# Moving evictions and two K jobs inside the attention pair loop of a fused two-layer kernel

## The reference

```python
x = x + tanh(g_xattn[0]) * L0_xattn(layernorm(x), ctx, ctx, mask, Wq, bq, Wk, bk, Wv, bv)
x = x + tanh(g_ffn[0])   * L0_ffn(layernorm(x), w1, w2, h1, h2, w3)          # ternary weights
x = x + tanh(g_xattn[1]) * L1_xattn(layernorm(x), ctx, ctx, Wq, bq, Wk, bk, Wv, bv, Wo, bo)
x = x + tanh(g_ffn[1])   * L1_ffn(layernorm(x), w_gate, w_up, w_down)        # rounded activations
# attention: scores = q @ k.T / sqrt(32); p = softmax(scores); out = p @ v, per batch and head
```

## Time and profile before

| what | value |
| --- | --- |
| median of three runs | 1588.3 us |
| the profiled execution | 1586.92 us |
| its span in the profile | 1584.5 us |
| PE busy | 1565.0 us, 99% |
| DVE, ACT, POOL busy | 1026.0, 971.0, 423.9 us |
| DMA, mean | 165 GB/s |

### The profile page before, as it was taken

One profiled execution on the slowest core, in us unless ns is written; L12 is line 12 of the kernel. 1 busy time (PEld: TensorE's weight loads), 2 busy tenths in 40 slices (PEclk: granted clock), 3 DMA queues, 4 the chain that ended last, 5 costly groups with the idle time before them and its releaser, 6 DMA issues.

```text
span 1584.5 us, 25762 instructions
## 1 busy us (share of the span) xinstructions
PE 1565.0 (99%) x9322; PEld 1427.5 (90%) x9322; DVE 1026.0 (65%) x1815; ACT 971.0 (61%) x2014; POOL 423.9 (27%) x569
## 2 busy tenths in 40 slices
PE   9999999999999999999999999999999999999999
PEld 7899899889888999999999998889999989988765
DVE  6577887787785563223544325647777777778987
ACT  5576777677665455444544435446677767666676
POOL 4121221222134222222222222311211121123751
PEclk9999999999999999999999999999999999999999
DMA  7766767677582325554365652576676677667500
GB/s 244 189 169 168 196 176 195 162 203 182 137 218 83 99 89 188 176 195 161 99 228 195 222 162 90 176 187 172 161 195 174 167 189 179 172 147 209 197 13 30
DMA packets 149974, 261.28 MB, mean 165 GB/s; under 512 B 41137, under 2 KB 94001, under 8 KB 149710
## 3 DMA queue, kind: packets, MB, share of 16 engines
q1 hardware_dynamic: 149505, 259.24, 58.3%
q10 hardware_dynamic: 332, 0.23, 0.0%
HBM read 191.01 MB, written 58.57 MB: 158 GB/s over the span
## 4 chain that ended last, share of the span: by engine, by line
PE 87%; DVE 6%; ACT 3%; DMA 2%; issue 1%; POOL 1%; SPq 0%; DVEq 0%; ACTq 0%
PE ps L1218 33%; PE ps L852 14%; PE ps L856 13%; PE ps L952 7%; PE ps L930 6%; PE ps L1152 2%; PE ps L1018 2%; PE ps L914 2%; PE ps L919 1%; DVE nmax L1367 1%; PE ps L1169 1%; PE ps L872 1%; ACT P L1909 1%; DVE PT L1373 1%; DMA kd<-ksl 1%
## 5 line engine op out<-in xcount | busy, mean ns | idle before, releaser
L1218 PE MATMUL ps<-ah_f,wh_f 128*128 128x400 f32 (+1 forms) x1296 | 442.9, 343 | 0.0
L1218 PE MATMUL ps<-al_f,wh_f 128*128 128x400 f32 (+1 forms) x1296 | 442.2, 342 | 0.0
L2272 POOL TENSOR_TENSOR cxl<-raw,cxh 128x384 fp32r<-128x384 f32 (+1 forms) x112 | 105.7, 965 | 562.7 <-ACT cxh L1851 562.7
L1773 DVE TENSOR_TENSOR wl_f<-raw_f,wh_f 128x1024 fp32r<-128x1024 f32 x85 | 103.7, 1223 | 231.9 <-POOL wh_f L2262 231.8
L1218 PEld LDWEIGHTS ps<-al_f,wh_f 128*128 128x128 f32 x1296 | 243.8, 188 | 0.0
L1218 PEld LDWEIGHTS ps<-ah_f,wh_f 128*128 128x128 f32 x1296 | 243.5, 188 | 0.1
L1367 DVE TENSOR_REDUCE nmax<-ps 100x1 f32<-100x722 f32 x256 | 220.6, 902 | 35.0 <-PE ps L918 31.4
L1909 ACT ACTIVATE P<-ps,nmax 100x722 f32<-100x722 f32 x256 | 219.9, 862 | 30.1 <-DVE nmax L1367 30.1
L1921 ACT ACTIVATE PT<-ps 128x400 fp32r<-128x400 f32 x384 | 165.9, 505 | 70.4 <-PE ps L930 69.2
L2190 ACT ACTIVATE raw_f<-wl_f 128x1024 f32<-128x1024 f32 x88 | 93.4, 1061 | 173.6 <-DVE wl_f L1773 173.0
L1373 DVE TENSOR_TENSOR PT<-ps,PT 128x400 fp32r<-128x400 f32 x384 | 196.3, 566 | 4.3 <-ACT PT L1921 1.1
(11 more groups left out here) (226 smaller groups left out, 2665.2 us busy)
## 6 DMA issues: line engine op xcount, KB each, us to landing
KS<-kd SPq DMA_DIRECT2D x192, 361.0 KB
raw_f<-in_h SPq DMA_DIRECT2D x64, 512.0 KB, 3.9
raw_f<-in_gud SPq DMA_DIRECT2D x48, 512.0 KB, 4.3
raw<-in_ctx SPq DMA_DIRECT2D x64, 192.0 KB, 3.6
raw_f<-in_w SPq DMA_DIRECT2D x24, 512.0 KB, 3.9
kd<-ksh SPq DMA_DIRECT2D x60, 192.0 KB, 2.2
kd<-ksl SPq DMA_DIRECT2D x60, 192.0 KB, 2.5
raw<-in_ctx SPq DMA_DIRECT2D x64, 169.0 KB, 4.5
```

Of the source, the lines that this page charges most:

```text
L1218: return e.matmul(o, p, q, start=start, stop=stop)
L1773: e.tensor_tensor(wl[:, z, :], raw[:, r, :], raw32(wh[:, z, :]), ALU.subtract).then_inc(v_ul, 1)
L2272: e.tensor_tensor(m.cx[1][:, k, off:off + n], m.raw[:, k, off:off + n], raw32(m.cx[0][:, k, off:off + n]), ALU.subtract).then_inc(g_cx, 1)
```

## The change

It has five parts.

1. `BESIDE[4]`: in pairs with `p == 4` K(2,0) comes first and K(0,1) second, before it was the other way. This holds for batches 1 to 7, so for seven pairs (4, 12, ... 52) in each layer, on every engine and in SyncE's stores.
2. The tail of batch 0 (and 1) is made in pair 0, behind K(3,1), in place of pair 1 ahead of its V job.
3. ScalarE evicts the tails of the other pairs (9, 17, 33, 41, 49 in both layers) between the two exponentials, not behind both.
4. The normalized rows of batch 5 are turned in pair 58, not 57; `normal_out` for them is in pair 57, not 56, and `keep_normal` in pair 58, behind both exponentials.
5. In pair 57 of the first layer VectorE does `low_weighed(55)` ahead of both maxima, not between them.

```diff
-          (("k", 1, 0, 1), ("k", 1, 2, 0)),
+          (("k", 1, 2, 0), ("k", 1, 0, 1)),
...
 def tail_at(i):
-    return i // 8 if i < NP and i % 8 == 1 and i // 8 % 4 < 3 else None
+    return i // 8 if i < NP and (i == 0 or i > 8 and i % 8 == 1) and i // 8 % 4 < 3 else None
...
     if i == NP - 1:
         return KEPT
-    return i // 8 - 2 if i % 8 == 1 and 16 < i < NP else None
+    if i == NP - 6:
+        return KEPT - 1
+    return i // 8 - 2 if i % 8 == 1 and 16 < i < NP - 8 else None
...
 # TensorE (JOBS, RINGS, VectorE and ScalarE: low_tail(0), high_tail(0) stand behind the jobs in the same way)
-                    if tail_at(i) is not None:
+                    if i and tail_at(i) is not None:
                         tail_job(tail_at(i))
                     for j in beside(i):
                         job(j)
+                    if i == 0:
+                        tail_job(0)
...
 # VectorE
-                    early = scaled_at(i) is not None or L == 0 and i < NP - 7 and (
-                        out_at(i) is not None or turned_at(i) is not None)
-                    between = L == 0 and i == NP - 7
+                    early = scaled_at(i) is not None or L == 0 and (i == NP - 7 or i < NP - 7 and (
+                        out_at(i) is not None or turned_at(i) is not None))
...
-                    if L == 0 and i == NP - 8:
+                    if L == 0 and i == NP - 7:
                         normal_out(i // 8 - 2)
...
 # ScalarE
                     if i + 1 < NP:
                         weights(2 * i + 2)
+                    if i and tail_at(i) is not None:
+                        high_tail(tail_at(i))
                     if len(beside(i)) < 2 and i + 1 < NP:
                         weights(2 * i + 3)
-                    if L == 0 and i == NP - 7:
+                    if L == 0 and i == NP - 6:
                         keep_normal(turned_at(i))
                     if L == 0 and i == NP - 1:
                         high_normal(KEPT)
-                    if tail_at(i) is not None:
-                        high_tail(tail_at(i))
...
                     for j in beside(i)[1:]:
                         high_job(j)
+                    if i == 0:
+                        high_tail(0)
```

More of the change, by code:

```diff
@@ L160 @@
     for _l in range(2):
-        if tail_at(_i) is not None:
+        if _i and tail_at(_i) is not None:
             JOBS[_l].append(("v", tail_at(_i), KT - 1))
         JOBS[_l] += beside(_i)
+        if _i == 0:
+            JOBS[_l].append(("v", 0, KT - 1))
         if scaled_at(_i) is not None:
@@ L169 @@
             RINGS[_l].append(("xn", turned_at(_i)))
-        if tail_at(_i) is not None:
+        if _i and tail_at(_i) is not None:
             RINGS[_l].append(("v", tail_at(_i), KT - 1))
         RINGS[_l] += beside(_i)
+        if _i == 0:
+            RINGS[_l].append(("v", 0, KT - 1))
         if _l and _i in OUT_AT:
@@ L1625, in attention @@
                         peak(2 * i + 2)
-                        if between:
-                            low_weighed(i - 2)
                         peak(2 * i + 3)
-                    if i >= 2 and not early and not between and (L == 0 or i < NP):
+                    if i >= 2 and not early and (L == 0 or i < NP):
                         low_weighed(i - 2)
@@ L1651, in attention @@
                         low_job(j)
+                    if i == 0:
+                        low_tail(0)
                     if L == 0 and out_at(i) is not None:
```

## The result

The kernel after takes 1592.41 us (median of 9 runs, 1590.87 to 1595.94), the kernel before 1587.81 (9 runs, 1585.70 to 1588.71): ratio 1.0033, 95% interval 1.0024 to 1.0043. It is slower by 4.6 us; forecast were 4.1 us more and 1592.4. The profiled execution took 1592.31 us with a span of 1589.9, before 1586.92 and 1584.5.

A forecast was written before the change was run, and what follows sets the result against it. TensorE is busy 99% of the span, so only edits moving a matmul's start count. Terms +9.3 - 1.7 - 1.4 - 1.2 - 0.9 = +4.1 us gave 1592.4 us, range 1586.5 to 1596.5.

The forecast's parts named there:

- Part 1, added: Pairs p = 4: K(2,0), now first, waits for K(1,0)'s store, issued behind spread_q, and delays the V product; +9.3 us.
- the nine named: Pairs forecast to stall: 4, 28, 36, 44 of the first layer; 4, 12, 28, 36, 44 of the second; 9.3 us.
- D - (end of job B) + 1.63: Stall cost in a pair p = 4, not under 0; D is when K(1,0)'s second transfer lands, job B the second K job.
- the six pauses: Pauses of about 1 us within SyncE's issues in six of nine stalling pairs, expected again; 6.0 us of the cost.
- The slow landings: Late-landing K(1,0) stores behind the other three stalls in pairs p = 4; 3.4 us, which may fall elsewhere.
- Rival (b): No change: pauses in SyncE's issues stay, slow landings do not; 6.0 - 5.2 = +0.8 us, 1589.1; chance 0.30.
- Part 1, removed: Stalls in pair 21 of the first layer and 53 of the second vanish as K(2,0)'s store leaves earlier; -1.7 us.
- Rival (c): Much slower: K(0,.) loads from p = 4 also miss pair 7, and pair 0's tail gains nothing; +10.5 us, 1598.8; chance 0.07.
- Part 2: Tail in pair 0: pair 2's transposes start at 72.0 instead of 72.69; 0.7 us in each layer, -1.4 us.
- Part 3: Pairs 17, 33, 41, 49 of the first layer: tail evicted earlier, V about 0.1 us late in pair 17; -1.2 us.
- Rival (d): The tails gain nothing since the second exponential becomes the late one; +1.2 us, 1593.6; chance 0.05.
- Parts 4 and 5: Pairs 57 and 58: V's 1.17 us wait goes, exponential starts 0.93 us earlier, next stage's weights move up too; -0.9 us.

The follow-up runs named there:

- experiment 2: Kernel before with only the K(2,0)/K(0,1) order swapped in pairs p = 4; 1598.34 us, ratio 1.0064 to before.
- Experiment 1: Kernel after with the order of K(0,1) and K(2,0) in pairs p = 4 put back as before; 1585.43 us, ratio 0.9989 to before.
- experiment 7: Kernel after with VectorE's half of pair 0's tail eviction moved behind the two maxima of pair 1; 1592.73 us, one run.
- Experiment 5: Kernel after with ScalarE's measure_low(0) one list entry later, behind pair 59's exponentials; 1592.04 us, one run.
- Experiment 6: Kernel before with ScalarE's measure_low(0) one list entry later; 1587.58 us, one run.
- experiment 4: Kernel after with four more transfers to a spare tensor between spread_q and K(1,0)'s store in each pair p = 3; 1630.51 us, ratio 1.0254 to before.
- Experiment 8: Kernel after with the K store ahead of three spread_q transfers, measure_low(0) later, and VectorE's pair 0 tail half behind pair 1's maxima; 1581.19 us, ratio 0.9951 to before.
- Experiment 9: Kernel of experiment 8 with the K jobs of pairs 4 and 5 in the order of the kernel before; 1582.04 us, ratio 0.9962 to before.
- experiment 3: Kernel after with three of spread_q's twelve transfers issued behind the K store; 1584.02 us, ratio 0.9977 to before.

## Why the prediction was right, and where it was not

**What bounds it.** Right: the work stayed, and only waits ahead of matmuls moved the time. The reading that a stall costs its pair's excess and not the idle time shown held in every case (pair 44: 1.57 idle, 1.73 longer).

**Part 1, added: +9.3 forecast, +8.4 measured.** Among the pairs with p = 4 the stalls fell in the nine named, and in no other over 0.15 us. The formula D - (end of job B) + 1.63, read with the landings of the kernel after, gives for the ten pairs where it is positive 1.34, 0.15, 0.34, 0.82, 1.83 and 1.10, 1.68, 0.97, 0.92, 0.46, together 9.6. The same pairs are longer than one without a stall by 1.34, 0.14, 0.33, 0.84, 1.83 and 1.10, 1.67, 1.00, 0.92, 0.45. What the sum left out: a pair with p = 4 that does not stall got 0.1 us shorter by the swap (7.22 to 7.12), in twelve pairs; that takes 1.2 us off. Of the 9.6, 4.6 stand in the five pairs with a pause in SyncE's issues and 4.9 in the four with a landing of 2.3 us or more. The chance in it was smaller than thought: four of the six pauses stayed (pairs 4 and 36, and 4 and 28 of the second layer), one shrank (pair 28: 1.16 forecast, 0.22 over the kernel before), and one was replaced by a slow landing (pair 36 of the second layer, 3.0 us). The slow landings, which I had taken for the part that may fall elsewhere, came back in place: pair 44 (3.9 us after, 3.95 in experiment 2) and pair 12 of the second layer (3.8 and 3.6). Rival (b) rested on their being rare and is refuted. What makes the pauses and the slow landings was not tested. Ten of the fourteen second transfers landed 2.06 to 2.09 us after their issue. The Trainium skill, "DMA: Bandwidth & Descriptors", section "Anatomy of one DMA", from which I had estimated 2.45 us, is for transfers issued by GpSimd. The estimate is 0.4 too slow for these and 1.5 too fast for the slowest (3.93), so the measurement decides: no one figure fits landings of 2.06 to 3.93 us of the same transfer.

**Part 1, removed: -1.7, measured -1.7** (0.72 and 1.00). Experiment 1 brought both back, so it is the order that removes them. load_k had its slack: in pair 20 its first transfer was issued 2.8 us later into the pair, within the forecast 1.2 to 3, and TensorE waited for it in no pair of the kernel after. Rival (c) did not happen.

**Part 2: -1.4, measured -1.2.** The chain is the one forecast, VectorE's eviction ahead of the two maxima; experiment 7 shows it by taking it away. Of the waits left, the 0.37 us before the second scores matmul was forecast, the 0.28 before the first was not.

**Part 3: -1.2, measured -0.9.** All four waits for the tail are gone, entirely, where 0.1 us was to stay; a late store put 0.7 us into pair 17 in this execution. Experiment 1 doesn't have it, and there the four pairs gain 1.6. Rival (d) did not happen.

**Parts 4 and 5: -0.9, measured +0.1. This step failed.** Two things went as forecast: pair 57's exponential starts 462.75 - 459.43 = 3.32 us after the pair's start, before 461.48 - 457.10 = 4.38, and V no longer waits 1.17 us there. The failing sentence is "the weights of the next stage (their fetch waits behind the store of K(3,1), which is 0.95 us earlier) move up too". Only the issue moved up. GpSimd (start, us, line), kernel before, with pair 57 from 457.10, then after, from 459.43:

```profile
464.30 1.04 POOL L2405 CAST wh_f<-raw_f 128x1024 fp32r<-128x1024 f32 x1 [6.35 <-DMA raw_f<-in_w]
465.42 2.39 POOL L2407 TENSOR_TENSOR wl_f<-raw_f,wh_f 128x1024 fp32r<-128x1024 f32 x1
```

```profile
466.69 1.04 POOL L2414 CAST wh_f<-raw_f 128x1024 fp32r<-128x1024 f32 x1 [6.41 <-DMA raw_f<-in_w]
467.81 2.39 POOL L2416 TENSOR_TENSOR wl_f<-raw_f,wh_f 128x1024 fp32r<-128x1024 f32 x1
```

The cast starts 7.20 and 7.26 us after the pair: the first of the four transfers took 4.6 us from issue to landing before and 5.7 after. Stretches of the kernel after (start:end, length, busy us of PE, PEld, DVE, ACT, POOL, then granted clock, DMA share, GB/s):

```profile
456.00:458.00 2.00, 2.00 (x17) 2.00 (x16) 1.90 (x6) 2.00 (x6) 0.00 (x0) 1.00 0.46 161
458.00:460.00 2.00, 2.00 (x14) 1.92 (x13) 1.99 (x4) 1.70 (x5) 1.29 (x2) 1.00 0.81 208
460.00:462.00 2.00, 2.00 (x24) 1.92 (x23) 1.89 (x5) 1.30 (x3) 0.28 (x1) 1.00 1.04 201
462.00:464.00 2.00, 1.19 (x12) 0.90 (x9) 1.97 (x4) 1.25 (x3) 0.00 (x0) 1.00 1.02 234
```

The DMA share is 1.0 from 460 on (0.6 us into the pair; before it is 1.04 from 457.70, as far in), with a load of K issued at 457.40 and the store ahead of the fetch; a transfer issued earlier only stands longer. Experiment 5 bears this out: the load of K went out 0.44 us later there, seen from pair 57's start, the fetch at the same 1.51 us, and its first transfer landed 7.71 us after that start, not 7.21. From there on a chain that the edit does not touch sets the time: GpSimd's remainder, measure_low on ScalarE (470.24 after, 467.84 before, 10.8 and 10.7 us into pair 57), the transposes' evictions, the exponentials of pair 59, the scores. These start 14.4 us after pair 57 in both kernels. The gain of pair 57 was wait changed for wait: 0.81 us before the scores and 0.49 before V in pair 58, which was forecast as 0.3 with nothing lost. Experiment 5 showed that measure_low is the cap. Experiment 6 showed what is under it: parts 4 and 5 then gain 0.73 us up to the end of pair 59, near the 0.9, but the load of K in pair 60 is the next cap and leaves 0.3.

**The sum.** +9.3 - 1.7 - 1.4 - 1.2 - 0.9 = +4.1, measured in the pairs +8.4 - 1.7 - 1.2 - 0.9 + 0.1 = +4.6. The swap was sized 0.9 too dear and the gains 1.5 too high. Start-up adds 0.7 in the profiled executions. That the median was hit (1592.41 for 1592.4) is luck: the kernel before was taken 0.5 us too high (1588.3, over nine runs 1587.81), the change 0.5 too low, and errors of 0.9 and 1.5 in the terms went against each other. Each term is right to 1 us.

## What to carry to other kernels

Where an instruction waits for a transfer, look at what the queue that issues it must issue first: here twelve transfers of 7.7 us ahead of one store, with pauses and slow landings on top, cost 8 us once the swap made a job wait for it, and sending the store ahead of three of them took all of it away. Before crediting a step with the time by which its inputs are issued earlier, look at the DMA share of that stretch: with full engines the landing stays where it was, and so does all behind it. And read a gain in one pair on to the next wait of the chain before it goes into the sum; here ScalarE, which works in order, waited there for GpSimd and took it back.

## What the runs showed of the hardware that was not expected

**A long wait can cost TensorE its clock.** In experiment 4, pair 28, TensorE waits 2.27 us for K(2,0), and after it the granted clock is 0.50 (1.2 GHz of 2.4). Stretches of that kernel, columns as above:

```profile
262.50:265.50 3.00, 3.00 (x20) 2.89 (x18) 2.27 (x5) 0.95 (x2) 0.00 (x0) 1.00 0.55 167
265.50:268.50 3.00, 0.72 (x5) 0.55 (x4) 0.62 (x1) 1.84 (x5) 0.00 (x0) 1.00 0.19 69
269.50:272.00 2.50, 2.50 (x14) 2.17 (x13) 1.62 (x2) 0.92 (x3) 0.00 (x0) 0.50 0.56 198
273.00:276.00 3.00, 3.00 (x20) 3.00 (x19) 2.23 (x5) 2.22 (x6) 0.00 (x0) 1.00 1.02 232
```

Pair 29, which waits for nothing, took 8.15 us for 6.78. There are eight such stretches in that kernel's span (clock 0.50 for 3.4 us, once 6.8), and none in those of the kernels before and after. Each starts within 1.7 us of the end of a stall of 1.6 to 3.7 us. It is not a matter of the wait alone: six of the 14 stalls, the longest 2.39 us, are followed by none. In the second layer, at pair 57, TensorE waited 1.26 and 1.25 us in the kernels of experiments 8 and 9; the first lost its clock, the second did not. That of experiment 3 waited 1.26 us there and lost it for 3.4 us. Experiment 8:

```profile
1451.00:1452.70 1.70, 0.43 (x3) 0.11 (x2) 1.57 (x5) 1.11 (x4) 0.00 (x0) 1.00 1.06 217
1453.00:1456.00 3.00, 2.63 (x14) 2.35 (x14) 2.95 (x6) 1.68 (x6) 1.08 (x1) 0.51 1.02 275
1456.00:1459.00 3.00, 3.00 (x11) 2.32 (x10) 2.21 (x6) 2.84 (x7) 1.80 (x2) 0.50 1.08 372
```

Experiment 9:

```profile
1451.00:1453.00 2.00, 0.93 (x6) 0.60 (x4) 1.90 (x5) 1.41 (x4) 0.00 (x0) 1.00 1.01 250
1453.00:1456.00 3.00, 2.45 (x17) 1.85 (x18) 2.97 (x6) 2.58 (x9) 1.09 (x1) 1.00 1.01 223
1456.00:1459.00 3.00, 3.00 (x15) 2.39 (x14) 2.65 (x7) 2.64 (x6) 0.95 (x1) 1.00 1.07 385
```

Pair 58 took 9.24 us there and 6.47 here: 2.8 us by the clock. This is part of the spread of the medians too. Of the kernel before, 19 executions with a mean granted clock of 1.000 took 1587.2 us on average, and 7 with 0.999 took 1588.8; of experiment 2, the two with 0.999 and 1.000 took 1596.2 and 1595.6, the three with 0.998 some 1598.6. So its median stands 2.8 us above its profiled execution: a stall can cost once by its length and once by the clock, and the second price is paid in some executions only. What decides it was not tested. A forecast made from an execution at full clock misses this part of the median.
